# Contextual attention on one core: feature buffers twice, their packs in mid-body, and a new order of the steps at a unit's end

## The chip, the core and the metric

The kernel runs on one core of one Trainium2 chip. The metric is the device time of one launch in microseconds: three timed runs before the change gave 1485.10, 1486.64 and 1486.96 us, median 1486.64. TensorE (PE in the profile) multiplies and transposes into PSUM, VectorE (DVE), ScalarE (ACT) and GpSimd (POOL) work on SBUF and PSUM, and SyncE (SP) issues nearly all DMAs.

## The reference

Two layers of the same function, each on four images of 64 channels and 80x80 pixels. The masks are inputs, all zero in the drawn data.

```python
def contextual(b, mask):                               # b: (4, 64, 80, 80)
    raw_w = patches(b, kernel=4, stride=2)             # 40*40 patches of 64*4*4
    w = patches(b[:, :, ::2, ::2], kernel=3, stride=1) # 40*40 patches of 64*3*3
    mm = (mean of the mask's 3x3 patches == 0)
    wn = w / max(sqrt(sum(w * w)), 1e-4)
    yi = einsum('bpd,bld->blp', w, wn) * mm            # scores, 1600 x 1600
    yi = softmax(yi * 10, axis=1) * mm
    p = einsum('blp,bld->bpd', yi, raw_w)
    out = the 4x4 patches p added up at stride 2, border cut
    return out / 4

x = contextual(x, L0_mask)
x = contextual(x, L1_mask)
```

## The kernel before, in words

**Units and tiles.** A unit is one image in one layer; there are eight, run one after the other. The image at half resolution, 40x40, is cut into three strips of 14 rows with a pitch of 41 (TW = 123 positions in a tile, TILES = 14 tiles). A unit's scores are a matrix G of 14 tiles by 14 blocks. G is symmetric up to shifts, so part of it is computed by `products` (L465, matmuls over fp16 features) and part is a transpose of what is stored (`transposes`, L474).

**Features.** Each value of the half-resolution image is split in fp16 into a high part and a low part. ScalarE writes the high part (`high_features`, L605 to L608) and VectorE the low part (`low_features`, L812 to L815) into `LOHI`: the low part in partitions 0 to 63, the high part in 64 to 127. SyncE then lays out four tiles of 128 partitions from it by eight DMAs (`packs`, `lay_out_features`, L299): HL (high over low), LH (low over high), H1 (high over high moved by one column) and HV (high over high moved by a row). The profile and the order below leave numbers out of names, so H1 stands there as H. Each of these four tiles and LOHI is there once, so the packs of the next unit can't start before all scores of the present one are made (SyncE waits for `g_ready` at step 28).

**Stages of a unit.** (1) Scores: TensorE fills psG, ScalarE copies the stored parts to G (`copy_scores`, L676; `copy_shared`, L663), VectorE adds the shared row product (L874), multiplies by the row scales RB and takes the maximum (`score_pair`, L880, L885), and ScalarE takes exponentials and their sums (`score_sums`, L690). (2) The logarithm of the softmax sum: `lse_max`, `lse_exp`, `lse_sum`, `lse_log` (ScalarE, L727), `lse_columns` (VectorE, L922, L924), then on TensorE `lse_row` (L400), a transpose that spreads it over rows in psB. It is made in two halves: tiles 0 to 3 at steps 23 and 24 (`second` False), tiles 4 to 13 at steps 28 and 29 (`second` True). (3) Arguments and softmax: VectorE makes scores minus logarithm (`argument_pair`, L934), ScalarE the exponential (`softmax_pair`, L701). (4) Shift: SyncE moves the result one partition on (`shift_pair`, L318, into SH), VectorE adds it (`add_shifted`, L945). (5) Sum: VectorE adds two neighbour tiles into Z (`sum_pair`, L967); for the first pair of a chunk one of the two sums (L963) needs a strip moved by DMA (`shift_strip`, L329, into SHJ), the other (L964) does not. (6) Paste: TensorE multiplies Z by blocks B of the raw image (`paste_tile`, L515) into psO, ScalarE reads it out (L710), SyncE stores it (`store_chunk`, L306). The blocks are transposed by TensorE (`block_group`, L446) and copied by ScalarE (L637).

**Order.** All of it is written out by hand. `body(u, v, w)` has 28 steps, s = 2 to 29. In it unit v has its scores made, unit u is pasted, and unit w is loaded. At step s the paste is that of place s, the sum that of s + 1, the added shift that of s + 2, the argument, exponential and shift that of s + 4; a place from 28 on is that of unit v, so steps 24 to 29 already run the first arguments of the next unit. A place is a chunk k (four of them) and a pair i of tiles (seven). Each engine runs its list strictly in this order and waits on semaphores. On SyncE's queue stand the shifts (four issues for a pair), the strips, the stores, the load of the next features (step 3, three DMAs of rows of 320 bytes), the load of the image (step 9, six such DMAs) and, at step 28, the eight packs. On VectorE at steps 28 and 29 the order is argument pair, add, sum, then the logarithm's operations.

## Time and profile before

| | before |
|---|---|
| median of three runs | 1486.64 us |
| time of the profiled execution | 1485.93 us |
| span of its profile | 1484.1 us |
| TensorE busy | 1340.5 us |
| VectorE busy | 1195.3 us |
| ScalarE busy | 853.7 us |
| granted clock of TensorE, mean | 0.973 |

The span is from the first instruction to the last; 1.8 us lie around it. The eight units overlap: the first body has scores only, the last one pastes only. The clock is a share of full speed. Busy shares are means over stages with different limits, so what a change is worth has to be read where the engines wait: from the waits, and from the timeline around the end of a unit.

### The profile page before, as it was taken

Reading aid. Unit: us, or ns where it says so; the run is one execution under the profiler, and the core shown is the slowest. Engines: PE = TensorE matmul, PEld = TensorE weight load, DVE = VectorE, ACT = ScalarE, POOL = GpSimd, SP = SyncE. Lnnn points to the kernel's source line nnn. Section 1 sums busy time; section 2 is a strip of 40 time slices with the busy share of each in tenths; the row PEclk is TensorE's granted clock in tenths of the full one; section 3 lists DMA queues with packets and bytes.
Section 4 is the critical chain, followed back from the end, with each engine's and each line's share of the span. In section 5 each row is a group of like instructions: output and inputs, shape, how many; then the busy total and the mean of one; then the engine's idle time right before and its main releaser. Section 6 shows DMA issues by size and latency. Waiting matters only on the chain.

```text
span 1484.1 us, 24228 instructions
## 1 busy us (share of the span) xinstructions
PE 1340.5 (90%) x7190; PEld 904.1 (61%) x7190; DVE 1195.3 (81%) x2830; ACT 853.7 (58%) x2233; POOL 47.6 (3%) x63
## 2 busy tenths in 40 slices
PE   4987999989999799998999899998999989999796
PEld 4765755667556675576656576566755666557343
DVE  4667889779888798878897878977888879888883
ACT  2667646656457564585555754666655755458431
POOL 1000000010000100001000000000000010000100
PEclk9997999999999999999999999999999999999999
DMA  5305462155622744137631556215462255412442
GB/s 101 45 1 133 108 130 70 51 150 116 127 61 65 172 101 109 52 85 165 122 93 34 130 128 136 78 44 143 119 124 72 62 143 113 111 51 83 129 137 57
DMA packets 181749, 146.57 MB, mean 99 GB/s; under 512 B 120114, under 2 KB 177522, under 8 KB 181618
## 3 DMA queue, kind: packets, MB, share of 16 engines
q1 hardware_dynamic: 181298, 144.04, 41.0%
q10 hardware_dynamic: 320, 0.99, 0.3%
q8 instruction: 57, 0.93, 0.3%
q14 instruction: 74, 0.61, 0.1%
HBM read 19.76 MB, written 13.11 MB: 22 GB/s over the span
## 4 chain that ended last, share of the span: by engine, by line
PE 32%; DVE 28%; SPq 11%; ACT 11%; issue 10%; DMA 7%; DVEq 0%; POOL 0%; ACTq 0%; POOLq 0%
PE psG L465 14%; PE psO L515 14%; DVE G L934 7%; DVE Z L967 5%; DVE G L874 4%; SPq L318 4%; DVE S L880 4%; DVE G L945 4%; ACT S L690 3%; ACT G L701 3%; SPq L299 3%; DMA HV<-LOHI 3%; PE psG L474 3%; ACT G L676 3%; DMA SH<-G 3%
## 5 line engine op out<-in xcount | busy, mean ns | idle before, releaser
L515 PE MATMUL psO<-Z,B 123*128 123x492 f32 (+2 forms) x1792 | 718.4, 530 | 38.5 <-DVE Z L967 25.2
L515 PEld LDWEIGHTS psO<-Z,B 123*128 123x128 f32 x1792 | 326.4, 194 | 238.1 <-issue 129.9
L465 PE MATMUL psG<-LH,HL 128*123 128x246 f16 (+2 forms) x2616 | 411.8, 287 | 38.2 <-DMA HV<-LOHI 28.7
L465 PEld LDWEIGHTS psG<-LH,HL 128*123 128x123 f16 x2616 | 280.5, 139 | 161.0 <-issue 96.7
L880 DVE CUSTOM_DVE_ANT_0 S<-G,RB 123x492 f32<-123x492 f32 (+1 forms) x448 | 269.1, 607 | 87.4 <-DVE G L874 55.0
L701 ACT ACTIVATE G<-G,nb 123x492 f32<-123x492 f32 (+1 forms) x448 | 267.0, 642 | 110.9 <-DVE G L934 110.4
L690 ACT ACTIVATE S<-S,nm 123x480 f32<-123x480 f32 (+3 forms) x560 | 307.3, 555 | 2.3 <-DVE nm L885 2.1
L945 DVE TENSOR_TENSOR G<-G,SH 123x492 f32<-123x492 f32 (+1 forms) x448 | 247.3, 591 | 54.2 <-DMA SH<-G 53.9
L934 DVE SCALAR_TENSOR_TENSOR G<-G,RA,psB 123x492 f32<-123x492 f32 (+1 forms) x448 | 270.1, 646 | 0.5 <-issue 0.5
L676 ACT ACTIVATE G<-psG 123x492 f32<-123x492 f32 (+3 forms) x256 | 120.1, 472 | 173.0 <-PE psG L465 92.5
L967 DVE TENSOR_TENSOR Z<-G 123x984 f32<-123x984 f32 (+2 forms) x192 | 197.3, 1028 | 0.6 <-PE psO L515 0.6
L465 PE MATMUL psG<-H 128*123 128x123 f16 (+3 forms) x872 | 195.7, 286 | 0.0
L663 ACT ACTIVATE G<-psG 123x246 f32<-123x246 f32 (+1 forms) x136 | 64.3, 472 | 227.7 <-PE psG L465 227.3
L874 DVE TENSOR_TENSOR G<-G,psG 123x492 f32<-123x492 f32 (+2 forms) x272 | 134.4, 494 | 73.2 <-ACT G L676 37.0
L474 PEld LDWEIGHTS psG<-idn,G 123*123 123x123 f32 x672 | 97.2, 195 | 68.5 <-ACT G L676 22.0
L474 PE MATMUL psG<-idn,G 123*123 123x123 f32 x672 | 112.4, 288 | 23.2 <-ACT G L676 14.2
L465 PEld LDWEIGHTS psG<-H 128*123 128x123 f16 x872 | 103.9, 138 | 21.0
L465 PE MATMUL psG<-HL 128*123 128x492 f16 (+2 forms) x392 | 112.5, 287 | 0.0
L690 ACT ACTIVATION_READ_ACCUMULATOR S<-S,nm 123x1 f32 x560 | 108.8, 194 | 0.0
L1076 POOL COPY G<-G 123x246 f32<-123x246 f32 x56 | 42.7, 770 | 1342.9 <-DVE mx L880 1175.9
L710 ACT ACTIVATE OSB<-psO 128x492 f32<-128x492 f32 (+2 forms) x64 | 31.5, 550 | 72.4 <-PE psO L515 72.3
L465 PE MATMUL psG<-HV 128*123 128x246 f16 (+2 forms) x240 | 68.4, 285 | 0.0
(83 smaller groups left out, 581.3 us busy)
## 6 DMA issues: line engine op xcount, KB each, us to landing
SH<-G SPq DMA_DIRECT2D x336, 214.8 KB
SH<-G SPq DMA_DIRECT2D x112, 89.2 KB
SH<-G SPq DMA_DIRECT2D x336, 19.2 KB
XP<-x SPq DMA_DIRECT2D x20, 280.0 KB, 5.9
XP<-mid SPq DMA_DIRECT2D x20, 280.0 KB, 5.3
HL<-LOHI SPq DMA_DIRECT2D x16, 246.5 KB, 3.5
mid<-OSB SPq DMA_DIRECT2D x48, 80.0 KB, 2.3
out<-OSB SPq DMA_DIRECT2D x48, 80.0 KB, 2.3
```

Source lines behind the costliest of these rows:

```text
L465: last = pe.matmul(psG[0:TW, bank, b0 * TW:b1 * TW], st[:, p:p + TW], mv[:, lo:lo + n], start=i == 0, stop=i == len(terms) - 1)
L474: last = pe.transpose(psG[0:TW, par, i * TW:(i + 1) * TW], G[:, c:c + TW], idn[0:TW, 0:TW])
L515: last = pe.matmul(psO[:, b, 0:n], B[:, o:o + 128], Z[:, 2 * (s % 2) + j, 0:n], start=t == 0, stop=t == TILES - 1)
L663: act.activation(to, psG[0:TW, FREE, stored * TW:w * TW], ACT.Copy).then_inc(p_copied, 1)
L676: act.activation(G[:, c:c + n], psG[0:TW, par, 0:n], ACT.Copy).then_inc(part if shared else read, 1)
L690: last = act.activation(y, y, ACT.Exp, bias=nm[:, k * TILES + t:k * TILES + t + 1], accum_out=sg[:, c:c + 1])
L701: act.activation(y, y, ACT.Exp, bias=nb[:, bass.ds(u * TILES + t, 1)]).then_inc(y_made, 1)
L874: dve.tensor_tensor((odd if par else even)[:, b0 * TW:n], rows[:, p0 * TW:p0 * TW + n - b0 * TW], psG[0:TW, par, b0 * TW:n], ALU.add).then ...
L880: dve.tensor_tensor_reduce(S[:, slot + par, 0:n], (odd if par else even)[:, 0:n], RB[:, s0 * TW:s0 * TW + n], 1.0, 0.0, ALU.mult, ALU.max, ...
L934: dve.scalar_tensor_tensor(out=g, in0=g, scalar=RA[:, bass.ds(u * TILES + t, 1)], in1=psB[0:TW, k % 2, 0:n], op0=ALU.mult, op1=ALU.subtrac ...
L945: dve.tensor_tensor(g, g, SH[:, o % SFREE, 0:n], ALU.add).then_inc(y1_made, 1)
L967: dve.tensor_tensor(Z[:, slot:slot + 2, 0:n], g[:, 2 * i:2 * i + 2, c0:c0 + n], g[:, 2 * i - 1:2 * i + 1, c0 - TW:c0 - TW + n], ALU.add).t ...
```

## The change

**Buffers.** LH, HL, H1 and HV get a second buffer each, chosen by the unit's parity. LOHI goes: ScalarE and VectorE write the high and low parts straight into LH, which has the same layout, and six packs instead of eight make HL, H1 and HV. HL, H1 and HV are no longer cleared at the start.

**Packs.** SyncE issues them at steps 10 (HL), 11 (H1) and 12 (HV) of the body in which the unit is loaded, each behind the shifts and strip of its step, and no longer at step 28. For the buffer to be free they wait for the scores of two units before; so does ScalarE's `high_features`.

**Order.** On VectorE, at steps 28 and 29, the add and the sum come ahead of the argument pair, and so do `lse_max` and `lse_sum`; `lse_columns` comes behind it. In the first pair of a chunk, the sum that needs the strip comes second, and only it waits. At step 24 ScalarE takes the logarithm ahead of the odd tile's copy, and TensorE the block's transposes ahead of the logarithm's row.

```diff
-        HL = sb("HL", [128, FLEN], F16)
-        LH = sb("LH", [128, FLEN], F16)
-        H1 = sb("H1", [128, FLEN], F16)
-        HV = sb("HV", [128, FLEN], F16)
+        LH = sb("LH", [128, 2, FLEN], F16)
+        HL = sb("HL", [128, 2, FLEN], F16)
+        H1 = sb("H1", [128, 2, FLEN], F16)
+        HV = sb("HV", [128, 2, FLEN], F16)
...
-        LOHI = sb("LOHI", [128, FLEN], F16)
-        LS, HS = LOHI[0:64, :], LOHI[64:128, :]
...
-        N_F = 8
+        N_F = 6
...
+        def halves_of(w):
+            return LH[0:64, w % 2, :], LH[64:128, w % 2, :]
...
             def lay_out_features(w, which):
+                if w >= 2:
+
+                    sp.wait_ge(g_ready, (w - 1) * NB)
+                    sp.sem_inc(sp_gate, 1)
                 sp.wait_ge(h_made, 2 * (w + 1))
...
-                    if s == SLOTS and w is not None:
-                        sp.wait_ge(g_ready, (v + 1) * NB)
-                        sp.sem_inc(sp_gate, 1)
-                        lay_out_features(w, ("HL", "LH", "H1", "HV"))
...
+                    if s in (10, 11, 12) and w is not None:
+                        lay_out_features(w, (("HL", "H1", "HV")[s - 10],))
...
-                    if s == 24 and v is not None:
-                        lse_row(v, w, 0)
...
                     if v is not None and 21 <= s < SLOTS - 1:
                         block_group(v, w, s - 21)
+                    if s == 24 and v is not None:
+                        lse_row(v, w, 0)
...
+                        if s == 24:
+                            lse_log(v, False)
                         copy_scores(u, v, j, 1)
                         if s == 23:
                             lse_exp(v, False)
-                        if s == 24:
-                            lse_log(v, False)
...
                 if i == 0:
-                    dve.tensor_tensor(Z[:, slot, 0:n], g[:, 0, c0:c0 + n], SHJ[:, 0:n], ALU.add)
-                    dve.tensor_tensor(Z[:, slot + 1, 0:n], g[:, 1, c0:c0 + n], g[:, 0, c0 - TW:c0 - TW + n],
-                                      ALU.add).then_inc(z_made, 1)
+                    dve.tensor_tensor(Z[:, slot + 1, 0:n], g[:, 1, c0:c0 + n], g[:, 0, c0 - TW:c0 - TW + n], ALU.add)
+                    dve.wait_ge(shj_in, (u * NK + k + 1) * 16 * len(STRIP_PARTS))
+                    dve.tensor_tensor(Z[:, slot, 0:n], g[:, 0, c0:c0 + n], SHJ[:, 0:n], ALU.add).then_inc(z_made, 1)
...
-                    if at and s != 24:
-                        if s == SLOTS + 1:
-                            lse_sum(v, True)
+
+                    if at and s != 24 and s < SLOTS:
                         argument_pair(at)
...
                     if s == SLOTS and v is not None:
                         lse_max(v, True)
+                    if s == SLOTS + 1 and v is not None:
+                        lse_sum(v, True)
+                    if at and s >= SLOTS:
+                        argument_pair(at)
                     if s == SLOTS + 1 and v is not None:
                         lse_columns(v, True)
```

What this does to the lists of three engines follows; line numbers are those of each kernel's own file.

SyncE before, at the end of the second body: the last shift of step 27, the eight packs (HL and LH two each in a row, H is H1), and the first shift of step 28.

```order
L318 DMA SH<-G 112x491
L318 DMA SH<-G 10x491
L299 DMA HL<-LOHI 64x1972 x2
L299 DMA LH<-LOHI 64x1972 x2
L299 DMA H<-LOHI 64x1972
L299 DMA H<-LOHI 64x1971
L299 DMA HV<-LOHI 64x1972
L299 DMA HV<-LOHI 64x1849
L318 DMA SH<-G 112x491
```

SyncE now, at steps 10 to 12 of the third body, from the last shift of step 10 to the first of step 12; LH is what the packs read. The two issues of HV follow behind step 12.

```order
L326 DMA SH<-G 10x491
L307 DMA HL<-LH 64x1972 x2
L326 DMA SH<-G 112x491
L326 DMA SH<-G 10x491
L326 DMA SH<-G 112x491
L326 DMA SH<-G 10x491
L307 DMA H<-LH 64x1972
L307 DMA H<-LH 64x1971
L326 DMA SH<-G 112x491
```

The packs moved from the unit's end, where they stood in one block, to three places between shifts, and are six instead of eight.

VectorE before, steps 28 and 29 (the arguments of place 32, add, sum, `lse_max`, `lse_sum`; then the same for place 33, and `lse_columns`).

```order
L934 SCALAR_TENSOR_TENSOR G<-G,RA,psB 123x492 x2
L945 TENSOR_TENSOR G<-G,SH 123x492 x2
L967 TENSOR_TENSOR Z<-G 123x2x369
L899 TENSOR_REDUCE nM<-nm 123x10
L901 TENSOR_TENSOR df<-nM,nm 123x4x10
L909 TENSOR_TENSOR sg<-sg 123x10
L914 TENSOR_TENSOR df<-ed,sg 123x4x10
L917 TENSOR_REDUCE tot<-df 123x10
L934 SCALAR_TENSOR_TENSOR G<-G,RA,psB 123x492 x2
L945 TENSOR_TENSOR G<-G,SH 123x492 x2
L967 TENSOR_TENSOR Z<-G 123x2x369
L922 TENSOR_TENSOR tot<-lns,nM 123x10
```

VectorE now, the same steps.

```order
L952 TENSOR_TENSOR G<-G,SH 123x492 x2
L971 TENSOR_TENSOR Z<-G 123x2x369
L906 TENSOR_REDUCE nM<-nm 123x10
L908 TENSOR_TENSOR df<-nM,nm 123x4x10
L941 SCALAR_TENSOR_TENSOR G<-G,RA,psB 123x492 x2
L952 TENSOR_TENSOR G<-G,SH 123x492 x2
L971 TENSOR_TENSOR Z<-G 123x2x369
L916 TENSOR_TENSOR sg<-sg 123x10
L921 TENSOR_TENSOR df<-ed,sg 123x4x10
L924 TENSOR_REDUCE tot<-df 123x10
L941 SCALAR_TENSOR_TENSOR G<-G,RA,psB 123x492 x2
L929 TENSOR_TENSOR tot<-lns,nM 123x10
```

Each argument pair (L934, now L941) moved behind the add and the sum of its step, and no add or sum stands any more between the second of them and `lse_columns`.

TensorE before, step 24: transposes of scores, paste, the logarithm's row, the transposes of a block, and the first scores of step 25.

```order
L474 MATMUL psG<-idn,G 123x123 x4
L515 MATMUL psO<-Z,B 128x328 x2
L400 MATMUL psB<-idn,lse 123x123 x4
L446 MATMUL psM<-idn,XP 123x128 x4
L474 MATMUL psG<-idn,G 123x123 x4
L515 MATMUL psO<-Z,B 128x328 x2
```

TensorE now, the same step.

```order
L480 MATMUL psG<-idn,G 123x123 x4
L521 MATMUL psO<-Z,B 128x328 x2
L452 MATMUL psM<-idn,XP 123x128 x4
L406 MATMUL psB<-idn,lse 123x123 x4
L480 MATMUL psG<-idn,G 123x123 x4
L521 MATMUL psO<-Z,B 128x328 x2
```

The row and the block's transposes have changed places.

## Rows read from the trace of the kernel before

**Rows 1.** Page, part 1: busy us (share of the span) xinstructions.

```profile
PE 1340.5 (90%) x7190; PEld 904.1 (61%) x7190; DVE 1195.3 (81%) x2830; ACT 853.7 (58%) x2233; POOL 47.6 (3%) x63
```

**Rows 2.** Waits, whole run: engine line <- releaser: us in total, times, longest.

```profile
DVE G L945 <- DMA SH<-G: 53.9, 28, 5.1
...
PE psG L465 <- DMA HV<-LOHI: 28.7, 7, 4.9
...
DVE Z L963 <- DMA SHJ<-G: 13.1, 13, 3.8
...
PE psG L465 <- DMA H<-LOHI: 0.9, 1, 0.9
```

**Rows 3.** Windows at seven unit ends: from:to length, busy us (xcount) per engine.

```profile
134.20:154.70 20.50, 14.97 (x73) 10.57 (x72) 14.69 (x35) 7.23 (x20) 3.54 (x5) 0.78 0.78 191
...
1197.03:1217.53 20.50, 14.42 (x81) 10.64 (x80) 15.05 (x35) 9.89 (x31) 3.54 (x5) 0.92 0.74 181
sum 143.50, PE 100.79 PEld 70.81 DVE 102.21 ACT 60.04 POOL 24.36; mean PE 14.40 PEld 10.12 DVE 14.60 ACT 8.58 POOL 3.48
```

**Rows 4.** Timeline, SyncE's queue at a unit end: start, us, what.

```profile
310.69 1.15 SPq L299 DMA_DIRECT2D HL<-LOHI  x2
...
317.80 7.57 SPq L318 DMA_DIRECT2D SH<-G  x8
...
325.41 3.91 SPq L306 DMA_DIRECT2D mid<-OSB  x6
```

**Rows 5.** Timeline, TensorE at the same unit end: [idle before <-releaser].

```profile
315.19 2.75 PE L515 MATMUL psO<-Z,B 123*128 123x369 f32 x8 [2.12 <-DVE Z L967]
...
322.27 1.46 PE L465 MATMUL psG<-LH,HL 128*123 128x246 f16 x6 [4.33 <-DMA HV<-LOHI]
```

**Rows 6.** Timeline, VectorE at the same unit end.

```profile
311.78 1.36 DVE L934 SCALAR_TENSOR_TENSOR G<-G,RA,psB 123x492 f32<-123x492 f32 x2
...
314.22 0.92 DVE L967 TENSOR_TENSOR Z<-G 123x738 f32<-123x738 f32 x1
...
322.98 1.30 DVE L945 TENSOR_TENSOR G<-G,SH 123x492 f32<-123x492 f32 x2 [1.71 <-DMA SH<-G]
...
329.80 0.28 DVE L874 TENSOR_TENSOR G<-G,psG 123x123 f32<-123x123 f32 x1 [3.37 <-ACT G L676]
```

**Rows 7.** Window behind the same unit end; PEclk is the figure after POOL.

```profile
322.20:327.00 4.80, 4.73 (x17) 3.94 (x18) 2.98 (x6) 1.56 (x3) 0.92 (x1) 0.50 0.49 142
```

**Rows 8.** Lines, two operations, whole run: busy us, mean ns | idle before.

```profile
L701 ACT ACTIVATE G<-G,nb 123x492 f32<-123x492 f32 (+1 forms) x448 | 267.0, 642 | 110.9 <-DVE G L934 110.4 <-issue 0.2
...
L964 DVE TENSOR_TENSOR Z<-G 123x492 f32<-123x492 f32 (+2 forms) x32 | 18.9, 591 | 0.0
```

**Rows 9.** Timeline, step 24 of one unit.

```profile
290.52 0.20 ACT L727 ACTIVATE lns<-tot 123x4 f32<-123x4 f32 x1
...
290.75 0.17 DVE L922 TENSOR_TENSOR tot<-lns,nM 123x4 f32<-123x4 f32 x1 [0.83 <-ACT lns L727]
...
291.26 0.66 PE L400 MATMUL psB<-idn,lse 123*123 123x123 f32 x4 [1.99 <-DVE lse L924]
...
292.65 2.64 DVE L934 SCALAR_TENSOR_TENSOR G<-G,RA,psB 123x492 f32<-123x492 f32 x4
```

**Rows 10.** Timeline, VectorE at step 5 of a later unit.

```profile
698.23 0.67 DVE L945 TENSOR_TENSOR G<-G,SH 123x492 f32<-123x492 f32 x1 [0.21 <-DMA SH<-G]
```

**Rows 11.** Timeline, SyncE and VectorE behind the image load, steps 9 to 13.

```profile
377.60 16.12 SPq L318 DMA_DIRECT2D SH<-G  x16
...
384.17 1.25 DVE L945 TENSOR_TENSOR G<-G,SH 123x492 f32<-123x492 f32 x2 [5.03 <-DMA SH<-G]
...
396.85 1.24 DVE L945 TENSOR_TENSOR G<-G,SH 123x492 f32<-123x492 f32 x2
```

**Rows 12.** DMA issues, two packs: xcount, KB each, median us to landing.

```profile
HL<-LOHI SPq DMA_DIRECT2D x16, 246.5 KB, 3.5
...
HV<-LOHI SPq DMA_DIRECT2D x7, 231.1 KB, 5.6
```

More of the change, by code:

```diff
@@ L297, in lay_out_features @@
                 sp.wait_ge(l_made, 2 * (w + 1))
-                for dst, src in packs(which):
+                for dst, src in packs(w, which):
                     sp.dma_start(dst, src).then_inc(f_in, 16)
@@ L497, in odd_tile @@
                 if alone > stored:
[L498 removed]
+                    products(v, j, 1, 1, stored, alone, TERMS)
                 if alone < w:
[L500 removed]
+                    last = products(v, j, 1, 1, alone, w, one_row(2))
                 last.then_inc(g_ready, 1)
@@ L783, in _ @@
             act.wait_ge(l_made, 2)
-            for dst, src in packs(("LH", "HV")):
+            for dst, src in packs(0, ("HV",)):
                 act.dma_start(dst, src).then_inc(f_in, 16)
```

41 lines of the change are left out of this document (19 added, 22 removed).

## The prediction

> **What bounds the kernel now.** I read the busy shares first, then the waits, then one unit end in order of time. TensorE is busy 90% of the span and VectorE 81% [rows 1]. Neither is the bound alone: inside a unit the two run side by side, nearly full, and time is lost at the unit ends. In the table of waits, TensorE waits 28.7 us in seven places for the transfer that lays out HV, and VectorE 53.9 us in 28 places for shifted columns [rows 2]. The seven places are the unit ends at which SyncE issues the eight packs of the next unit. In a window of 20.5 us around each, VectorE is busy 14.6 us in the mean and TensorE 14.4 us [rows 3]: 5.9 us of VectorE's time is idle at every unit end.
>
> At the one at 311 us the order is this. SyncE issues packs from 310.69 and reaches its next shifts only at 317.80 [rows 4]. TensorE pastes at 315.19 after 2.12 us idle, and then idles 4.33 us until HV has landed at 322.27 [rows 5]. VectorE idles 1.71 us for the shift that left SyncE late, and 3.37 us for a score copy that TensorE's late start held back [rows 6]. After its 4.33 us of idleness TensorE works from 322.2 to 327.0 at a granted clock of 0.50, the lower level of 1.2 GHz [rows 7].
>
> **Part 1, the packs leave the unit end.** Removed: eight issues of SyncE (310.69 to 317.8, 7.1 us of its queue) and TensorE's wait for them. Two of the eight, LH's, vanish, since LH is now written by the engines themselves. TensorE wins its 4.33 us and the doubled time at 0.50, but this doesn't set the gain, because VectorE follows right behind. Of VectorE's 5.9 us idle, about 0.9 are short gaps between dependent instructions and stay (5.9 less 1.7 and 3.4, rounded). So 5.0 us can go.
>
> **Part 2, the new order on VectorE at steps 28 and 29.** No work is added. Before, the argument pair at 311.78 ran ahead of the sum at 314.22 [rows 6]. It costs two times 0.65, so this sum is ready 1.3 us earlier, and the paste of 315.19 starts at about 314.0. At step 29 the order is now sums, lse_sum, argument pair, lse_columns, and this makes a wait. ScalarE takes the two exponentials of that pair (0.64 us each [rows 8]) ahead of the logarithm (0.20 us [rows 9]), for which lse_columns waits. Before, an add and a sum of VectorE covered this; now nothing does. One exponential, the logarithm and two handovers of 0.1 make 1.05 us of new idle time. Behind it are queued lse_columns and the next arguments, and on TensorE the row of the second chunk, which then waits some 1.7 us; TensorE is far enough ahead for that. Left per unit end: 5.0 - 1.05 = 3.95 us.
>
> **What is late next.** SyncE. From 311.78 VectorE now has add, sum and maxima (2.6 us), arguments (1.3), add and sum (2.1), lse_sum (0.6) and the first argument (0.65): 319.1. An exponential later, at 319.8, the shift leaves, and after four issues of 0.7 us the store that started at 325.41 [rows 4] starts at 322.6. SyncE gains 2.8 us where VectorE gains 3.95. Behind that store stand the load of features and the first shift of the next chunk. At 698.23 VectorE already waits 0.21 us for such a shift [rows 10]; there the 1.15 us of difference are lost. It is the only unit with a wait there, so the others have some time to spare. I take off 1.3 us in all: 7 x 3.95 - 1.3 = 26.4 us. Bounds: 35 (7 x 5.0, no log wait), and 14, if the log wait, the row and SyncE take half.
>
> **Part 3, packs in mid-body.** Six issues (HL at step 10, H1 at 11, HV at 12) go between shifts on SyncE, 5.3 us of its queue (six eighths of 7.1) in three portions. There, after the image load, shifts are issued from 377.60 on, four pairs in 16.12 us, and VectorE waits 5.03 us at 384.17 for the first of them [rows 11]. The first pack comes behind the second pair. By an even share of the 16.12 us the third pair has left by 389.7, and with a pack ahead by 391.5; it is used at 396.85 [rows 11]. Packs land in 3.5 (HL) to 5.6 us (HV's second half) [rows 12]. HL, the one ahead of this pair, makes it 395.0; that is before the use. The strip and the fourth pair are needed later still. So I cost this part at nothing: it lies beside arguments and sums. Without that cover it costs up to 5.6 us per pack.
>
> [...]
>
> **Part 4, step 24.** ScalarE's logarithm for the first tiles stood at 290.52, behind a copy that waits for a sum. VectorE waited 0.83 us for it at 290.75, and TensorE 1.99 us for the row at 291.26 [rows 9]. Now the logarithm comes before that copy, at 288.8. VectorE's wait goes, and TensorE transposes a block in its own. The arguments at 292.65 [rows 9] start 0.85 us earlier (0.83, and the row behind it alike). ScalarE's exponentials, its copy of the block and the strip's transfer all follow from them, so it is passed on. Eight units: 6.8 us. Bounds 3 and 9.
>
> **Part 5, the strip's sum second.** The other sum, 0.59 us [rows 8], fills the wait for the strip: 13 waits, 13.1 us, the longest 3.8 [rows 2]. A wait gives its own length, but at most 0.59, so the bounds are 1.5 us and 7.7 (13 x 0.59). With a longest of 3.8 most of the 13 must be short: I take 4.1 us, a little over half of 7.7.
>
> **Part 6, the two ends.** At the start TensorE waits 0.9 us for the H1 pack [rows 2]; with two packs fewer in flight it goes: 0.9 us. The memsets that go lie beside the first load and give nothing. The eighth unit end has no packs, so there only costs are left: the log wait of 1.05 us, and arguments of step 29, and so a shift, that come about 2 us later. I take -1.6.
>
> **Sum.** 26.4 + 6.8 + 4.1 + 0.9 - 1.6 = 36.6 us. The profiled execution took 1485.93 us, 0.7 under the median of 1486.64. From it the sum gives 1449.3, from the median 1450.0. I say 1450.
>
> **The rivals.** A is the forecast, 1443 to 1458.
>
> B, the wait moves and does not go. The log wait, TensorE's wait for the row, and SyncE's late store and feature load take back more than I counted. For it: SyncE's lead is only 2.8 us. If a unit end gives 1.5 to 2.5 us instead of 3.8, and parts 4 to 6 give 7 instead of 10, the gain is 10.5 to 17.5 and 7: 1462 to 1469. Mixed cases lie between.
>
> C, TensorE decides and not VectorE. Then a unit end gives its 4.33 us, 1.2 of the 2.12, half of the 4.8 us at 0.50, less the 1.7 for the row: 6.2 us, seven times 43.4 instead of 26.4: 1433, with part of it up to 1443. For it: TensorE is the busier engine over the span. Against it: at the unit end VectorE has little more idle time than it has named waits. The Trainium skill ("TensorE: Matmul & The Clock Gate", section "HAM oscillation — how this bites in real kernels") tells of waits on a DMA after which matmuls run at half clock. By that rule, the trace agrees, the slow stretch goes with the wait.
>
> D, slower: the packs collide with the shifts, at steps 10 to 13. If the queue still holds image rows when the first pack is issued, and the three packs (3.5 + 5.6 + 5.6, some 14 us of landing) act as one block ahead of the third pair, it lands at 391 + 14 = 405, 8 us after its use, and 12 if the strip suffers too. Seven units: 56 to 84 us against the 37 gained, 1506 to 1534. It decides from 5.2 us per unit. Against it: the first pair lands at 384.17 behind all of the image rows, and the packs are issued in three steps some 6 us apart.
>
> E, the change doesn't do what it says: SyncE's waits ahead of the packs (features made, scores of two units before) hold until the unit's end. Features are made at steps 5 and 6, so they should not. 1478 to 1488.
>
> **How the numbers follow.** A 0.62, B with the mixed cases 0.20, C 0.10, D 0.04, E 0.04. The range takes in A, most of B and the upper part of C: 1440 to 1466. What a measurement of this kernel tells from no change is about 0.2%, 3 us. Faster by more: A, B, C and half of E, 0.94. Same: half of E and a mild D, 0.03. Slower: 0.03.
>
> **What would show it.** In the profile after, TensorE's wait for HV (28.7) should be gone, and with it the clock of 0.50 behind a unit end. VectorE should wait about 1.0 us for the second logarithm at each of eight unit ends, and not at step 24. Its wait for shifts should fall from 53.9 to about 43, by 1.5 us or so at each unit end, with short new ones at the first shift behind the feature load. The wait of 5 us behind the image load should stay; if it grows, or new ones stand at steps 12 to 14, part 3 is wrong. The period from unit to unit is 177.1 us now (a sixth of the way from 134.2 to 1197.0 [rows 3]) and should be near 172. I am wrong if VectorE has little idle time left at the unit ends and the period still falls by less than 3 us.

## The result and the profile after

The changed kernel takes 1452.28 us (median of four runs, 1446.61 to 1452.71) against 1486.80 of the kernel before in the same session: ratio 0.976, 95% interval 0.9733 to 0.9786. The gain is 34.5 us where 36.6 were predicted; 1450 was forecast, 1440 to 1466 the range. The profiled execution took 1452.71 us, its span is 1450.9 us (1484.1 before).

The page's first part, busy time of each engine (answers to [rows 1]): the same work in a shorter span.

```profile
PE 1327.8 (92%) x7190; PEld 890.1 (61%) x7190; DVE 1192.4 (82%) x2827; ACT 854.9 (59%) x2233; POOL 53.4 (4%) x62
```

The waits of the whole run, total us, times, longest (answers to [rows 2]):

```profile
DVE G L952 <- DMA SH<-G: 51.9, 32, 5.0
PE psB L406 <- DVE lse L931: 17.1, 14, 2.1
...
DVE tot L929 <- ACT lns L734: 8.2, 9, 1.2
DVE Z L969 <- DMA SHJ<-G: 7.6, 5, 3.0
```

TensorE's wait for HV is gone. The strip's wait fell from 13.1 to 7.6 us. The logarithm's wait stands there as foreseen: 8.2 us in nine places, 1.0 us at seven of the eight unit ends and 1.2 at one. The period from unit to unit is 172.7 us, where 172 was foreseen (a sixth of the way from 128.39 to 1164.36, where the first and the seventh unit end start). But VectorE's wait for shifts fell by 2 us only, in 32 places instead of 28, where I had expected 43 us.

I compare stretches between marks of VectorE's work, since they leave out what differs at the start. The **unit end** runs from the argument pair of step 27 to that of step 3 of the next unit, with its steps 28 and 29; **behind it** is the stretch from there to the first shifted add of the second chunk, the first whose shift stands behind the feature load. The windows of the kernel before at its seven unit ends, with packs (from:to length, busy us (xcount) of PE, PEld, DVE, ACT, POOL, then clock, DMA share, GB/s), the first and the sum:

```profile
129.09:153.78 24.69, 17.25 (x91) 12.10 (x90) 18.45 (x44) 11.83 (x34) 3.54 (x5) 0.79 0.70 178
...
sum 174.41, PE 127.27 PEld 91.49 DVE 129.00 ACT 88.08 POOL 24.36; mean PE 18.18 PEld 13.07 DVE 18.43 ACT 12.58 POOL 3.48
```

The same of the changed kernel (answers to [rows 3]):

```profile
299.53:320.06 20.53, 17.47 (x114) 12.72 (x113) 18.51 (x44) 13.03 (x38) 4.32 (x5) 1.00 0.35 99
...
1164.36:1184.95 20.59, 17.46 (x114) 12.71 (x112) 18.56 (x44) 12.98 (x38) 4.32 (x5) 1.00 0.34 98
sum 145.76, PE 122.12 PEld 88.57 DVE 129.79 ACT 90.36 POOL 30.32; mean PE 17.45 PEld 12.65 DVE 18.54 ACT 12.91 POOL 4.33
```

VectorE's busy time is nearly the same (129.0 and 129.8); the stretches are 28.65 us shorter in all, 4.1 each. The clock is 1.00 in five of them and 0.92 in two, where it was 0.79 to 0.93. Now the stretch behind it, first of before, then after:

```profile
sum 83.07, PE 83.07 PEld 68.81 DVE 76.76 ACT 42.44 POOL 12.95; mean PE 11.87 PEld 9.83 DVE 10.97 ACT 6.06 POOL 1.85
```

```profile
sum 88.20, PE 88.20 PEld 71.57 DVE 76.57 ACT 51.50 POOL 12.92; mean PE 12.60 PEld 10.22 DVE 10.94 ACT 7.36 POOL 1.85
```

Here 5.13 us are given back, with VectorE's work unchanged. Of 28.65 us, 23.5 are left. The other parts: step 24 (arguments of step 23 to those of step 24, seven units) went from 68.49 to 61.72 us, 6.8; the body where the packs now are (arguments of step 11 to those of step 16) from 221.23 to 222.29; of the remaining 4 of the 33.2 us between the spans, 2.4 lie between the stretch behind the unit ends and the arguments of step 8, 0.7 in the start, and the rest is spread.

The new unit end in order of time, from the changed kernel's timeline at 311 us (start, us, engine, instruction, idle before it and its releaser), VectorE first:

```profile
305.32 1.43 DVE L952 TENSOR_TENSOR G<-G,SH 123x492 f32<-123x492 f32 x2
306.68 1.11 DVE L971 TENSOR_TENSOR Z<-G 123x738 f32<-123x738 f32 x1
...
308.06 1.36 DVE L941 SCALAR_TENSOR_TENSOR G<-G,RA,psB 123x492 f32<-123x492 f32 x2
...
312.21 1.35 DVE L941 SCALAR_TENSOR_TENSOR G<-G,RA,psB 123x492 f32<-123x492 f32 x2
314.52 0.17 DVE L929 TENSOR_TENSOR tot<-lns,nM 123x10 f32<-123x10 f32 x1 [0.96 <-ACT lns L734]
```

ScalarE, TensorE and SyncE there (answers to [rows 4 to 6]):

```profile
313.04 1.34 ACT L708 ACTIVATE G<-G,nb 123x492 f32<-123x492 f32 x2 [2.19 <-DVE G L941]
314.29 0.19 ACT L734 ACTIVATE lns<-tot 123x10 f32<-123x10 f32 x1
```

```profile
307.84 2.75 PE L521 MATMUL psO<-Z,B 123*128 123x369 f32 x8 [0.82 <-DVE Z L971]
...
315.04 0.66 PE L406 MATMUL psB<-idn,lse 123*123 123x123 f32 x4 [1.73 <-DVE lse L931]
```

```profile
301.64 14.89 SPq L326 DMA_DIRECT2D SH<-G  x12
316.57 3.90 SPq L314 DMA_DIRECT2D mid<-OSB  x6
320.57 2.83 SPq L326 DMA_DIRECT2D SH<-G  x4
323.52 2.10 SPq L270 DMA_DIRECT2D XP<-x  x3
325.73 8.76 SPq L326 DMA_DIRECT2D SH<-G  x9
```

The pair of arguments at 312.21 is that of step 29. Its exponentials end at 314.4; only then come the logarithm, for which VectorE sits idle, and the shift, behind which SyncE's store, four shifts and the feature load (XP<-x, 323.52) wait. The next shifts, issued from 325.73, are those that the stretch behind the unit end waits for.

### The profile page after: what moved, and what is told of

Its sections match the earlier page's. It is cut to its first block, busy times and chain, and to the rows that moved or that the text cites. A ratio compares the mean times of both kernels' runs of the same rounds, so it can differ in the third digit from the quotient of the medians.

```text
span 1450.9 us, 24200 instructions
## 1 busy us (share of the span) xinstructions
PE 1327.8 (92%) x7190; PEld 890.1 (61%) x7190; DVE 1192.4 (82%) x2827; ACT 854.9 (59%) x2233; POOL 53.4 (4%) x62
## 4 chain that ended last, share of the span: by engine, by line
DVE 41%; PE 20%; issue 13%; SPq 9%; ACT 9%; DMA 6%; DVEq 1%; POOL 0%; ACTq 0%; POOLq 0%
DVE G L941 10%; PE psG L471 9%; PE psO L521 8%; DVE Z L971 7%; DVE G L881 6%; DVE S L887 6%; DVE G L952 5%; DMA SH<-G 5%; SPq L326 4%; SPq L270 3%; ACT G L708 3%; ACT S L697 3%; ACT G L683 2%; PE psG L480 2%; SPq L314 2%
## 5 line engine op out<-in xcount | busy, mean ns | idle before, releaser
L521 PE MATMUL psO<-Z,B 123*128 123x492 f32 (+2 forms) x1792 | 709.2, 524 | 30.4 <-DVE Z L971 20.9
L521 PEld LDWEIGHTS psO<-Z,B 123*128 123x128 f32 x1792 | 321.4, 192 | 227.4 <-issue 121.0
L471 PEld LDWEIGHTS psG<-LH,HL 128*123 128x123 f16 x2616 | 276.7, 137 | 145.2 <-issue 65.3
L941 DVE SCALAR_TENSOR_TENSOR G<-G,RA,psB 123x492 f32<-123x492 f32 (+1 forms) x448 | 269.9, 645 | 0.0
L1082 POOL COPY G<-G 123x246 f32<-123x246 f32 x56 | 49.4, 897 | 1305.6 <-DVE mx L887 1170.1
```

The costliest lines, as they stand in the source:

```text
L471: last = pe.matmul(psG[0:TW, bank, b0 * TW:b1 * TW], st[:, v % 2, p:p + TW], mv[:, v % 2, lo:lo + n], start=i == 0, stop=i == len(terms) - 1)
L521: last = pe.matmul(psO[:, b, 0:n], B[:, o:o + 128], Z[:, 2 * (s % 2) + j, 0:n], start=t == 0, stop=t == TILES - 1)
L941: dve.scalar_tensor_tensor(out=g, in0=g, scalar=RA[:, bass.ds(u * TILES + t, 1)], in1=psB[0:TW, k % 2, 0:n], op0=ALU.mult, op1=ALU.subtrac ...
```

## The experiments

The theory taken to the chip: behind the packs, the next thing late at a unit end is SyncE's queue, and the new order of steps 28 and 29, which makes the arguments of step 29 late, costs more there than it brings. The rival: the order is worth its 1.3 us a unit end and only the logarithm's wait stands against it. All times are medians in us. The kernels were timed in groups, each beside the kernel before, whose median was between 1484.6 and 1487.6 in these groups; the ratios are to the one of the same group. The last two columns are sums over seven units, from one profile of each kernel.

| kernel | time | ratio to before, 95% | unit end, 7 | behind it, 7 |
|---|---|---|---|---|
| before | 1486.8 | | 174.41 | 83.07 |
| changed | 1452.3 | 0.9733–0.9786 | 145.76 | 88.20 |
| packs alone | 1448.4 | 0.9734–0.9768 | 140.27 | 84.43 |
| orders alone | 1477.1 | 0.9928–0.9967 | 173.37 | 83.06 |
| changed, arguments first | 1437.8 | 0.9664–0.9693 | 135.57 | 84.00 |
| changed, logarithm first | 1446.3 | 0.9723–0.9752 | 138.38 | 91.77 |
| changed, feature load behind | 1447.9 | 0.9718–0.9758 | 144.62 | 81.84 |
| changed, new order at step 28 alone | 1446.1 | 0.9709–0.9750 | 144.78 | 84.08 |
| arguments first, load behind | 1435.4 | 0.9636–0.9677 | 135.36 | 82.39 |
| arguments first, strip's sum as before | 1438.4 | 0.9649–0.9701 | 139.15 | 83.67 |
| step 24 alone | 1477.4 | 0.9917–0.9956 | 175.93 | 83.08 |
| changed, packs ahead of shifts | 1453.1 | 0.9758–0.9801 | 144.68 | 87.28 |
| arguments first, both loads behind | 1422.5 | 0.9552–0.9598 | 136.37 | 82.20 |
| the same, packs at steps 13 to 15 | 1418.7 | 0.9519–0.9582 | 135.27 | 82.17 |

**Packs alone.** The buffers and mid-body packs stay; the orders of step 24, of the strip's sum and of steps 28 and 29 are those of before (the minus lines of the change come back for these three, as here for the strip's sum).

```diff
+                if i == 0:
+                    dve.wait_ge(shj_in, (u * NK + k + 1) * 16 * len(STRIP_PARTS))
...
-                    dve.tensor_tensor(Z[:, slot + 1, 0:n], g[:, 1, c0:c0 + n], g[:, 0, c0 - TW:c0 - TW + n], ALU.add)
-                    dve.wait_ge(shj_in, (u * NK + k + 1) * 16 * len(STRIP_PARTS))
-                    dve.tensor_tensor(Z[:, slot, 0:n], g[:, 0, c0:c0 + n], SHJ[:, 0:n], ALU.add).then_inc(z_made, 1)
+                    dve.tensor_tensor(Z[:, slot, 0:n], g[:, 0, c0:c0 + n], SHJ[:, 0:n], ALU.add)
```

> The changed kernel with its reordering undone: the order of step 24, of the strip's sum and of steps 28 and 29 is that of before; the feature buffers and the mid-body packs stay. Prediction's parts: 1, 3 and 6 alone, that is 7 x 5.0 = 35 us at most, less what SyncE's queue takes back (it gains 2.8 us a unit end where VectorE gains 5.0: 7 x 2.2 = 15 at most, if every unit waits there as the one at 698 us does), plus 0.9 at the start: 21 to 36 us under before, 1451 to 1466. Theory (after the change SyncE's queue behind the unit end is the next bound, so the order matters little): the packs bring about 25 us, 1461. Rival (the orders bring a third of the gain or more): 1466 or above.

Measured 1448.4, under both numbers: the packs' move alone is worth 37 us by the medians. That is more than the whole change, but 3.5 us of it are an earlier start in its profile, whose cause is open (last section); behind the start its span is only 1.6 us shorter than the changed kernel's. Its unit ends:

```profile
sum 140.27, PE 121.75 PEld 90.95 DVE 126.97 ACT 90.88 POOL 24.51; mean PE 17.39 PEld 12.99 DVE 18.14 ACT 12.98 POOL 3.50
```

174.41 less 140.27 are 34.1 us, 4.9 a unit end: nearly all of the 5.0 that I had called removable. Behind it 1.4 us are given back (84.43 against 83.07). Most of the rest, 4.2 us against the kernel before, is the start.

**Orders alone.** The kernel before with the three reorderings and the packs at the unit's end.

> The kernel of before with the reordering alone (step 24, strip's sum, steps 28 and 29); the eight packs stay at the unit's end. Theory: step 24 gives its 7 to 8 us, the strip's sum 1 to 4, and the order of steps 28 and 29 nothing, since VectorE waits there for the sums behind the packs in any case: 1475 to 1479. Rival (sums ahead of arguments are worth 1.3 us a unit end by themselves, because TensorE's paste starts earlier): 9 us more, 1466 to 1470. If the late shift pair of step 29 costs, because the packs stand in the same queue: 1480 or above.

Measured 1477.1: the theory's. The unit ends hardly move (173.37), and TensorE's wait for the packs grows from 28.7 to 37.1 us:

```profile
PE psG L465 <- DMA HV<-LOHI: 37.1, 7, 5.8
```

**Arguments first.** The changed kernel, VectorE's order at steps 28 and 29 undone.

```diff
-                    if at and s != 24 and s < SLOTS:
+                    if at and s != 24:
+                        if s == SLOTS + 1:
+                            lse_sum(v, True)
                         argument_pair(at)
...
-                    if s == SLOTS + 1 and v is not None:
-                        lse_sum(v, True)
-                    if at and s >= SLOTS:
-                        argument_pair(at)
```

> The changed kernel with VectorE's old order at steps 28 and 29 (arguments ahead of maxima and sums), all else as changed. Theory (SyncE's queue is the next bound at a unit end: the arguments of step 29, and with them a shift pair, the store and the feature load, come late because of the new order): the time stays or falls, 1445 to 1453, the table of waits shows no VectorE wait for the second logarithm at step 29, and the short waits for the shift behind the feature load (0.7 to 2 us in six units) shrink. Rival (the earlier sums are worth 1.3 us or more at each unit end, as the prediction's part 2 has it): slower by 8 to 10 us, 1460 to 1462.

Measured 1437.8, 14.4 us faster than the change and below the theory's range. Unit ends and the stretch behind, windows of this kernel:

```profile
sum 135.57, PE 116.09 PEld 84.75 DVE 126.67 ACT 90.66 POOL 24.65; mean PE 16.58 PEld 12.11 DVE 18.10 ACT 12.95 POOL 3.52
...
sum 84.00, PE 84.00 PEld 68.25 DVE 76.56 ACT 48.10 POOL 12.95; mean PE 12.00 PEld 9.75 DVE 10.94 ACT 6.87 POOL 1.85
```

10.19 us (145.76 - 135.57) are in the unit ends and 4.20 (88.20 - 84.00) behind them: 14.4, the whole difference; the other stretches differ by 1.2 us at most and cancel, and the starts are level. So the new order costs 2.05 us a unit. Only the part behind, less than a third, is where the theory looked for it, in SyncE's queue. Of the 10.19, VectorE's busy time takes 3.12 (129.79 - 126.67) and idle time the other 7.1, which is about the seven logarithm waits (7 x 0.96 = 6.7). In this kernel VectorE doesn't wait for that logarithm:

```profile
309.92 1.34 ACT L708 ACTIVATE G<-G,nb 123x492 f32<-123x492 f32 x2 [0.76 <-DVE G L941]
311.17 0.20 ACT L734 ACTIVATE lns<-tot 123x10 f32<-123x10 f32 x1
...
312.36 0.39 DVE L929 TENSOR_TENSOR tot<-lns,nM 123x10 f32<-123x10 f32 x1
```

The exponentials and the logarithm lie beside an add and a sum of VectorE, and the store starts at 313.90 and not at 316.57, 0.6 us of it because the unit itself is that much earlier.

**Logarithm first.** The changed kernel, ScalarE's order at step 29.

```diff
+                    if s == SLOTS + 1 and v is not None:
+                        lse_log(v, True)
                     if at and not pairs:
                         softmax_pair(at)
                     if s == SLOTS and v is not None:
                         lse_exp(v, True)
-                    if s == SLOTS + 1 and v is not None:
-                        lse_log(v, True)
```

> The changed kernel with ScalarE's logarithm of step 29 ahead of the softmax pair of that step, all else as changed. VectorE waits 8.2 us for that logarithm in nine places in the changed kernel. Theory (SyncE's queue decides at the unit end): the 8.2 us of waiting go, but the shift pair then leaves 0.2 us later and VectorE meets the shift behind the feature load earlier, so its wait there grows by about as much: 1450 to 1453, no change. Rival (VectorE's own sum of work and waits decides, as the prediction counted the log wait at 1.05 us a unit end): 8 us faster, 1444.

Measured 1446.3, 5.9 us faster: between the two, nearer to the rival. The unit ends give 7.4 us (145.76 - 138.38), the stretch behind takes 3.6 back (91.77 - 88.20), and the wait for shifts grows by 3.3 us, as the theory had it, but this eats half of the gain and not all of it:

```profile
DVE G L952 <- DMA SH<-G: 55.2, 31, 5.0
```

Against the kernel with the arguments first, 7.8 us are lost behind the unit ends (91.77 against 84.00) and 2.8 in them, 2.5 of these as busy time of VectorE. With the logarithm's wait out of the way, what the late arguments cost is mostly in SyncE's queue.

**Feature load behind the shift.** The changed kernel, on SyncE:

```diff
-                    if s == 3 and w is not None:
-                        load_features(u, w, feat_src)
                     at = place(u, v, s + LEAD)
                     if at:
                         shift_pair(at)
+                    if s == 3 and w is not None:
+                        load_features(u, w, feat_src)
```

> The changed kernel with SyncE's load of the next features moved behind the shift pair of its step (step 3), all else as changed: SyncE then issues the first shift of the second chunk one transfer earlier. In the changed kernel VectorE waits for that shift in six units (0.9, 1.5, 1.0, 2.1, 1.3 and one more), some 6 to 7 us in all. Theory (SyncE's queue behind the unit end takes part of the gain back there): those waits go, 1445 to 1447. Rival (the waits stand for something else, TensorE's or VectorE's own lateness, and would turn up a few instructions later): 1451 to 1453.

Measured 1447.9, 4.4 us faster, 0.9 above the theory's 1445 to 1447; the rival's was 1451 to 1453. The stretch behind the unit end is 81.84 us, 11.69 in each of the seven, with no wait left, and the wait for shifts is 6.1 us shorter:

```profile
sum 81.84, PE 81.84 PEld 65.51 DVE 76.12 ACT 46.77 POOL 12.95; mean PE 11.69 PEld 9.36 DVE 10.88 ACT 6.68 POOL 1.85
```

So what the change gives back behind its unit ends is a shift that stands behind the feature load in SyncE's queue. That this profile's span is only 4.4 us shorter comes mostly from its last unit, 3.1 us longer at a lower clock (last section).

**Both together.** Arguments first and the feature load behind the shift.

> The changed kernel with two edits: VectorE's old order at steps 28 and 29 (1437.8 us by itself), and the feature load behind the shift pair of step 3. With the old order the stretch from the arguments of step 3 to the first shifted add is 12.0 us in the mean against 11.7 in the unit without a load. Theory (with the arguments early again SyncE has nearly caught up, and only 0.3 us a unit are left there): 1435 to 1438. Rival (the load is a cost of its own, whatever the order): 6 us less, 1431 to 1433.

Measured 1435.4, as the theory had it. With the arguments early again only 1.6 us (84.00 - 82.39) were left behind the load. VectorE's wait for shifts is 43.4 us in this kernel, what the forecast had said of the changed one.

**New order at step 28 alone.** Step 29 as before.

```diff
-                    if at and s != 24 and s < SLOTS:
+                    if at and s != 24 and s != SLOTS:
+                        if s == SLOTS + 1:
+                            lse_sum(v, True)
                         argument_pair(at)
...
-                    if s == SLOTS + 1 and v is not None:
-                        lse_sum(v, True)
-                    if at and s >= SLOTS:
+                    if at and s == SLOTS:
                         argument_pair(at)
```

> The changed kernel with the new order at step 28 alone (sum and maxima ahead of the arguments); step 29 as before (sum of exponentials, arguments, add, sum, then the columns). It tells which half of the new order costs the 14 us between the changed kernel (1452.3) and the one with the old order at both steps (1437.8). Theory (the loss is at step 29: the logarithm's wait of 1.05 us and the shift pair of step 29 that comes 2 us later): within 3 us of the old order, 1436 to 1441. Rival (the late arguments of step 28 already make the softmax row, the shift and the store late): half or more of the loss stays, 1444 to 1450. The prediction's own term, a paste of TensorE that starts 1.3 us earlier: below 1436.

Measured 1446.1: the rival's, my reading that the loss is all at step 29 falls. The median makes this kernel look better than it is, since its profile starts 3.8 us earlier. By the stretches, 9.2 of the 10.2 us in the unit ends are there with the new order at step 28 alone (144.78 against 135.57), while the stretch behind them is as with the arguments first (84.08 and 84.00): the order at step 28 costs the unit end, the one at step 29 costs SyncE's queue. The waits of this kernel show what takes the logarithm's place:

```profile
DVE df L921 <- ACT ed L729: 7.3, 8, 0.9
```

With the arguments late at step 28, the pair's exponentials stand ahead of the small exponential ed on ScalarE, and VectorE waits 0.9 us for that. With the order at both steps the add and sum of step 29 cover it, and the logarithm is left uncovered. Either way one pair of exponentials in each unit end lies in front of a small result for which VectorE waits.

**The strip's sum.** Arguments first, and the strip's sum first again as in the kernel before (the lines shown at packs alone).

> The changed kernel with VectorE's old order at steps 28 and 29 (1437.8 us by itself), and the strip's sum first again as before: the difference to 1437.8 is what the strip's sum second is worth. The prediction took 4.1 us (bounds 1.5 and 7.7): 1439 to 1445. By the stretches of the traces, in which step 24 gives nearly all of what the two give together (0.9 us a unit, 7 of the 10.6 us between packs alone and this order): 1438 to 1441.

Measured 1438.4 against 1437.8, with runs from 1433.9 to 1441.5. By the medians nothing can be told. By the unit ends, in which the strip's wait lies, it is 3.6 us (139.15 - 135.57), and this kernel's start is 3.3 us earlier in its profile (last section). I take 3.6 with that reserve. Behind the start as a whole, this kernel's span is 2.3 us longer: its waits for the strip are 6.0 us longer (14.1 and 8.1), but its waits for shifts are 4.5 shorter (42.6 and 47.1).

**Step 24 alone** on the kernel before.

```diff
-                    if s == 24 and v is not None:
-                        lse_row(v, w, 0)
...
                         block_group(v, w, s - 21)
+                    if s == 24 and v is not None:
+                        lse_row(v, w, 0)
...
+                        if s == 24:
+                            lse_log(v, False)
                         copy_scores(u, v, j, 1)
                         if s == 23:
                             lse_exp(v, False)
-                        if s == 24:
-                            lse_log(v, False)
```

> The kernel of before with the new order of step 24 alone (ScalarE's logarithm ahead of the score copy, TensorE's row behind its block); packs at the unit's end, all else as before. The prediction's part 4: 8 x 0.85 = 6.8 us (bounds 3 and 9), 1478 to 1482 against 1486. Rival (the 0.83 us of waiting only moves to the next wait for scores): 1484 or above. Together with the kernel that has all reorderings (1477.1) it bounds what the other two are worth without the packs' move: 2 us or less if the stretches of the traces are right.

Measured 1477.4, 9 to 10 us faster, more than foreseen. Packs alone against the kernel with the same orders but step 24's (1448.4 and 1438.4) gives 10.0 again. The stretch of step 24 itself gives 6.7 in seven units (68.49 to 61.76). This kernel's profile can't show the rest, since the profiled execution took 1480.0, the longest of its six, 5.9 us under the one of before. In the other pair the starts are level and the spans 10.3 us apart (1445.8 and 1435.5): 6.4 are in the seven stretches of step 24, 1.9 at the unit ends and behind them, and 2.8 in the last unit, whose length differs by as much between profiles of kernels that are alike there (last section). The kernel with all reorderings (1477.1) is no faster than this one by the medians: without the packs' move the others bring nothing that can be told, though its seven unit ends are 2.6 us shorter in the profiles.

**Packs ahead of the shifts** of their steps, in the changed kernel.

```diff
+                    if s in (10, 11, 12) and w is not None:
+                        lay_out_features(w, (("HL", "H1", "HV")[s - 10],))
                     at = place(u, v, s + LEAD)
                     if at:
                         shift_pair(at)
...
-                    if s in (10, 11, 12) and w is not None:
-                        lay_out_features(w, (("HL", "H1", "HV")[s - 10],))
```

> The changed kernel with the packs of steps 10 to 12 ahead of the shift pair of their step and not behind it: each shift pair there leaves two issues (1.8 us) later and has one pack more ahead of it. Prediction's part 3 puts the lead of the third pair at about 2 us with a pack ahead of it. Theory (the packs lie beside other work with a lead of a few us to spare): the pair whose lead is smallest now has a pack more ahead of it, 0 to 2 us a unit, 1452 to 1466, and the loss stands as a wait for shifted columns or for the strip between steps 9 and 14. Rival D (packs and shifts act as one block in the queue): each pair waits for the packs' whole landing, 3.5 to 5.6 us more in every unit, 1475 or above.

Measured 1453.1, 0.8 us slower by the medians and 2.8 by the ratios to before (0.9779 and 0.9760), whose intervals overlap. The stretch of steps 11 to 16, of the changed kernel and of this one:

```profile
sum 222.29, PE 212.65 PEld 117.29 DVE 205.37 ACT 104.74 POOL 0.00; mean PE 30.38 PEld 16.76 DVE 29.34 ACT 14.96 POOL 0.00
```

```profile
sum 224.83, PE 213.69 PEld 117.32 DVE 205.56 ACT 104.75 POOL 0.00; mean PE 30.53 PEld 16.76 DVE 29.37 ACT 14.96 POOL 0.00
```

2.5 us in seven units, 0.36 each, where rival D had 3.5 to 5.6 each. There is time to spare around the packs.

**Both loads behind.** Arguments first, feature load behind the shift, and the image load of step 9 moved behind the shift pair and the strip in the same way.

```diff
-                    if s == 9 and v is not None:
-                        load_image(u, w, image_src)
                     at = place(u, v, s + LEAD)
...
                     if at and at[2] == 0:
                         shift_strip(at)
+                    if s == 9 and v is not None:
+                        load_image(u, w, image_src)
```

> The changed kernel with three edits: VectorE's old order at steps 28 and 29, the feature load behind the shift pair of step 3 (these two together gave 1435.4), and the image load behind the shift pair of step 9. VectorE waits about 5 us in seven units for the first shift behind the image load, 35 us in all. If the image rows ahead of that shift in the queue are the cause: that wait goes, but the strip and the pairs of the next steps then have the image rows ahead of them instead; up to 35 us faster, 1400, and by my estimate half of that, 1418. If the wait only moves to the next pair: 1433 to 1438. If the rows, the packs and the last pairs collide: slower, 1440 to 1460.

Measured 1422.5, 12.9 us faster than without the image load's move, close to my estimate. From the arguments of step 8 to those of step 11, and on to those of step 16, seven units, without the move:

```profile
sum 162.69, PE 162.69 PEld 106.27 DVE 125.33 ACT 86.10 POOL 0.00; mean PE 23.24 PEld 15.18 DVE 17.90 ACT 12.30 POOL 0.00
...
sum 221.87, PE 213.29 PEld 117.43 DVE 205.44 ACT 105.52 POOL 0.00; mean PE 30.47 PEld 16.78 DVE 29.35 ACT 15.07 POOL 0.00
```

and with it:

```profile
sum 131.16, PE 131.16 PEld 86.28 DVE 124.76 ACT 65.96 POOL 0.00; mean PE 18.74 PEld 12.33 DVE 17.82 ACT 9.42 POOL 0.00
...
sum 238.89, PE 238.82 PEld 136.77 DVE 207.16 ACT 120.66 POOL 0.00; mean PE 34.12 PEld 19.54 DVE 29.59 ACT 17.24 POOL 0.00
```

The first is 31.5 us shorter, the wait of 5 us is gone there. The second is 17.0 longer, and TensorE is busy in 238.82 of 238.89 us. Before, it did 31.5 us more of its work in the first stretch, beside VectorE's wait, and then had 8.6 us idle in the second; now it is the bound. So of the 35 us that the wait seemed worth 14.5 are left over the two stretches (31.5 less 17.0).

**Packs at steps 13 to 15,** in that kernel.

```diff
-                    if s in (10, 11, 12) and w is not None:
-                        lay_out_features(w, (("HL", "H1", "HV")[s - 10],))
+                    if s in (13, 14, 15) and w is not None:
+                        lay_out_features(w, (("HL", "H1", "HV")[s - 13],))
```

> The version of 1422.5 us (VectorE's old order at steps 28 and 29, feature load and image load behind the shift pair of their step) with the packs at steps 13, 14 and 15 and not at 10, 11 and 12: they no longer stand in the queue between the image rows and the strip. There VectorE still waits about 1.3 us a unit for the first shifts of the third chunk and 1 us for the strip, and the stretch from the arguments of step 11 to those of step 16 is 34.1 us against 31.7 without the image load moved. Theory (in this crowded stretch the packs, hidden elsewhere, hold up the strip and a pair): the waits for shifts and strip shrink, 1 to 2 us a unit, 1408 to 1416. Rival (the packs lie beside other work here too, and the image rows or TensorE make the 34.1): 1420 to 1425.

Measured 1418.7 (1415.7 to 1422.6), between the theory's range and the rival's. It is the lowest median of all, but its interval overlaps with the one ahead, and the two spans are 1419.3 and 1419.4 us, this one with a start that is 2.7 us later. The strip's wait fell from 10.8 to 7.0 us and the stretch of steps 11 to 16 only from 238.89 to 237.17, with TensorE busy throughout. That is 0.25 us a unit and not 1 to 2: the rival's mechanism, with TensorE as the bound.

## Why the prediction was right, and which term was mis-sized

**Part 1, right.** 5.0 us a unit end were called removable, and packs alone gave 4.9. (The gaps that stay are 0.8 us by the forecast's own rows, 5.9 less 1.71 and 3.37, and not 0.9, which changes nothing.) The clock followed: around the changed kernel's unit ends it is 1.00 in five of seven. At the one of 311 us TensorE idles 0.82 us and 1.73 us, and not 4.33. In the other two a short slow stretch is left, which I had expected to go everywhere: TensorE idles 2.08 us ahead of 136.69 and 2.02 us ahead of 488.73, and the granted clock is then 0.50 from 138 to 140 and from 490 to 492.

**Part 2, right mechanism, size too small.** The forecast put the logarithm's wait at 1.05 us; it is 0.96. What it left out is in the words "No work is added". First, VectorE's busy time at the unit end is 0.45 us longer than with the arguments first (3.12 / 7), mostly by a contention that no step of mine had (last section). Second, the sum that is ready earlier brought nothing that shows: the kernel without it is 14.4 us faster. TensorE was 0.82 us idle ahead of its paste even so, and then waited 1.73 us for the row.

**What is late next, right place, too small.** I named SyncE's store and feature load and took 1.3 us off in all. They took 5.1. The step that failed is "It is the only unit with a wait there, so the others have some time to spare": five of the seven stretches behind a unit end are 0.8 to 2.1 us longer than the 11.69 of one without a wait. The 1.15 us of difference was too small as well: at the unit end of 311 us it was 1.9. The store starts 17.04 us behind the first arguments of this unit end instead of 19.82, so SyncE gained the 2.8 us of the forecast, but VectorE gained 4.7 us (25.26 - 20.53) and not 3.95. At 507 us, for one, VectorE waits 0.65 and 0.24 us for the first two shifts. Parts 1 and 2 with this gave 19.9 us instead of 26.4 (23.5 less the strip's 3.6).

**Part 3, right.** The stretches with the packs are unchanged to 0.15 us a unit, and even a pack ahead of each shift pair cost 0.4 us a unit. D fell: packs and shifts don't act as one block there. E fell too: in the third body the three packs are issued at 374.60, 379.35 and 385.78 us.

**Part 4, a little small.** 6.8 us in eight units, 0.85 each; measured 6.8 in the stretches of seven, 0.97 each, and 9 to 10 by the medians.

**Part 5, near.** 4.1; 3.6 by the unit ends, 2.3 by the span behind the start, and 0.6 by the medians, which can't tell it from nothing.

**Part 6, right.** The eighth unit end went from 17.83 to 18.55 us and the stretch behind it from 8.83 to 9.78: 1.7 lost, 1.6 foreseen. The span doesn't show the loss, since what follows in that unit is 1.8 us shorter (90.35 and 92.18), at a clock of 0.95 and 0.93, which the forecast didn't have. TensorE's wait for the H1 pack is gone, and the first unit end starts 0.7 us earlier; but the clock at the start differs too (last section), so the 0.9 isn't shown.

The errors partly cancelled: 6.5 too much at the unit ends, up to 3 too little at step 24. B was nearer to the truth than its chance says: the new order and SyncE's queue took back 15 us (10.2 in the unit ends, of which 3.1 are the contention that B didn't have either, and 5.1 behind them) where the sum had 8.7. It stayed within A because the packs gave all of their 5 us, and by luck: 2.4 us ahead of step 8 and 1.8 in the last unit came in places for which the sum had nothing. C fell: TensorE isn't full at the unit ends (122.12 of 145.76 us).

## What to carry to other kernels

Where one engine feeds three others, ask of an order what it makes late on each of them, and not only on the engine that waits visibly. Here the arguments ahead of the sums were worth 14 us: about 7 as a small result of ScalarE for which VectorE no longer waited, 4 in SyncE's queue of shift, store and load, and 3 as busy time beside GpSimd's copies. Before moving a large instruction past a small one, look on every engine for a small result that then stands behind it, and for what covered it. And undo each part of a change that wins: here the new order of steps 28 and 29 cost 14 of the 49 us that the rest was worth. A wait is worth its length only until the next engine is full; look at that engine's busy time in the stretch behind it.

## What the runs showed of the hardware

**VectorE and GpSimd hold each other up.** GpSimd copies columns of G (the wraps) at the unit end. With the arguments first, two of these copies lie beside an argument pair; in the changed kernel three lie beside the add and the sum. GpSimd's timeline, arguments first, then the changed kernel:

```profile
304.94 0.73 POOL L1079 COPY G<-G 123x246 f32<-123x246 f32 x2 [148.64 <-DVE mx L887]
307.37 0.93 POOL L1079 COPY G<-G 123x246 f32<-123x246 f32 x1 [1.71 <-DVE G L952]
```

```profile
305.56 2.47 POOL L1082 COPY G<-G 123x246 f32<-123x246 f32 x3 [147.83 <-DVE mx L887]
```

A copy takes 0.37 us beside the argument pair and 0.82 in the changed kernel. (The one at 307.37 lies beside the sum, takes 0.93 us, and leaves the sum at its 0.92.) The argument pair takes 1.36 us with and without copies beside it; the add pair grows from 1.24 to 1.43 us and the sum from 0.92 to 1.11. The Trainium skill ("GPSIMD Engine Reference", section "Specifications") says that GpSimd's SBUF interface is shared with VectorE, with contention when a VectorE instruction has two SBUF inputs. The trace agrees: the add and the sum have two tiles in SBUF as inputs, while one of the arguments' tensors is in PSUM. These 0.38 us a unit are most of the 3.1 us of busy time by which the changed kernel's unit ends exceed those with the arguments first. The eleven kernels with the packs in mid-body bear it out: VectorE's busy time in the seven unit ends is 129.2 to 129.9 us in the five with the new order at step 28, and 126.6 to 127.2 in the others. No run moves the copies alone, so the cause rests on the time that the two engines spend side by side.

**The clock at the start and the end.** All kernels run the same work up to the end of the first unit's scores, but for the order of step 24; yet the argument pair of the first unit's step 27 starts at 128.39 us in the changed kernel's profile and at 128.19 with arguments first, but at 124.90 with packs alone and 124.55 with the new order at step 28 alone. The granted clock differs there. TensorE's windows (length, busy, clock, DMA share, GB/s) of the changed kernel and of packs alone:

```profile
60.00:90.00 30.00, 26.95 (x150) 0.94 0.20 48
90.00:125.00 35.00, 28.68 (x157) 0.80 0.10 28
```

```profile
60.00:90.00 30.00, 26.74 (x165) 1.00 0.18 43
90.00:125.00 35.00, 28.28 (x167) 0.85 0.14 40
```

The last unit differs too. From the last arguments of step 24 to the end it takes 131.61 us at a mean clock of 0.96 in the changed kernel and 134.74 at 0.93 with the feature load behind, though no features are loaded there. One profile of each kernel doesn't tell whether this goes with the kernel or with the run; but the changed kernel alone was timed at 1446.6 and three times at 1452.1 to 1452.7. So differences below some 4 us between two of these kernels are read from the stretches, not from the medians.
